# Two of three PSUM banks change owner, and the order of the attention steps is made anew

## What is computed

```python
q = rope((x @ Wq + bq).reshape(B, 512, 16, 16))       # 16 heads of 16
k = rope((x @ Wk + bk)[:, :, None, :])                # one key head for all
v = (x @ Wv + bv)[:, :, None, :]
att = softmax(where(causal, -inf, einsum('bthd,bThd->bhtT', q, k) / sqrt(16)))
x = x + ga * (einsum('bhtT,bThd->bthd', att, v).reshape(B, 512, 256) @ Wo + bo)
h = layernorm(x) * (1 + cb) + sb                      # and the router's logits of h
```

## Time and profile before

| | |
|---|---|
| median of 3 runs | 1330.33 us (1328.81 to 1330.93) |
| the profiled execution | 1328.92 us, of which 1327.0 us span |
| mean granted TensorE clock | 0.924 of full |
| attention, from the first transposes of the input to the last logits | 44.8 to 507.2 us |
| busy over the span | PE 84%, DVE 56%, ACT 43%, POOL 34% |

### The profile page before, as it was taken

The page is one execution under the profiler, slowest core; times in us unless marked ns, Lnnn a source line. Parts: engine busy times, 40 slices in busy tenths (PEclk is TensorE's granted clock), DMA queues, the critical chain, the costliest instruction groups (busy, mean ns, idle before and its releaser), DMA issues. The chain is left out here.

```text
span 1327.0 us, 19347 instructions
## 1 busy us (share of the span) xinstructions
PE 1121.3 (84%) x6462; PEld 593.2 (45%) x6462; DVE 744.3 (56%) x1538; ACT 566.0 (43%) x1025; POOL 457.4 (34%) x668
## 2 busy tenths in 40 slices
PE   6279999999999991598989638999999929999996
PEld 5134445554544430354545315666666613333332
DVE  3167778788787745223223237777777623464543
ACT  0227676676776661123223213333333204545543
POOL 0345446445454310478877523222223100000000
PEclk7669999999999995699999859999999969999997
DMA  4134134233252213266666430111110020012000
GB/s 169 30 58 77 26 70 93 46 75 85 39 90 58 43 50 105 72 128 155 130 151 132 75 99 1 37 37 37 37 41 17 21 91 1 8 56 64 0 32 32
DMA packets 73042, 85.26 MB, mean 64 GB/s; under 512 B 12520, under 2 KB 67560, under 8 KB 72688
## 3 DMA queue, kind: packets, MB, share of 16 engines
q1 hardware_dynamic: 60656, 67.23, 19.8%
q0 software_dynamic: 12288, 16.79, 7.7%
HBM read 45.54 MB, written 25.47 MB: 54 GB/s over the span
## 5 line engine op out<-in xcount | busy, mean ns | idle before, releaser
L655 DVE TENSOR_REDUCE nmax<-psum 128x1 f32<-128x512 f32 (+3 forms) x352 | 215.5, 636 | 51.9 <-PE psum L847 46.5
L759 ACT ACTIVATE pT<-psum 128x512 f32<-128x512 f32 x320 | 181.1, 596 | 66.7 <-PE psum L866 36.6
L845 PE MATMUL psum<-k6T,q6T 96*128 96x512 bf16 (+3 forms) x512 | 128.2, 310 | 14.3 <-DVE nmax L655 10.2
L863 PE MATMUL psum<-q6T,k6T 99*128 99x512 bf16 x320 | 119.4, 382 | 1.1 <-ACT pT L759 0.9
L1084 POOL DMA_INDIRECT residual<-expert_y,idx_e x64 | 101.2, 1581 | 37.6 <-DVE expert_y L1206 21.1
L2029 PE MATMUL psum<-c_state,c_w 128*128 128x512 f32 x192 | 102.5, 636 | 0.1
L847 PE MATMUL psum<-negs_bf,ident_bf 128*128 128x128 bf16 (+2 forms) x352 | 88.8, 252 | 0.0
L845 PEld LDWEIGHTS psum<-k6T,q6T 96*128 96x128 bf16 x512 | 45.7, 99 | 88.0 <-DVE nmax L655 55.5
L878 PE MATMUL psum<-pT,v 128*32 128x512 f32 x640 | 85.1, 604 | 0.0
L1487 DVE TENSOR_TENSOR l_scores<-psum,const_sb 128x512 f32<-128x512 f32 x128 | 79.1, 679 | 10.0 <-PE psum L1639 10.0
L1071 POOL DMA_INDIRECT expert_tokens<-router_input,idx_e x64 | 63.7, 995 | 54.3 <-POOLq L947 35.2
(11 more groups left out here) (234 smaller groups left out, 2259.1 us busy)
## 6 DMA issues: line engine op xcount, KB each, us to landing
q6T<-q_parts SPq DMA_DIRECT2D x96, 128.0 KB, 4.5
expert_w<-in_ew SPq DMA_DIRECT2D x16, 768.0 KB
x_in<-in_x SPq DMA_DIRECT2D x8, 512.0 KB, 4.0
residual<-x SPq DMA_DIRECT2D x32, 128.0 KB, 1.8
router_input<-h SPq DMA_DIRECT2D x32, 128.0 KB, 1.8
l_x<-residual SPq DMA_DIRECT2D x8, 512.0 KB, 4.2
x_dram<-l_x SPq DMA_DIRECT2D x32, 128.0 KB, 3.5
c_x<-x_dram SPq DMA_DIRECT2D x4, 1024.0 KB, 6.0
```

The lines of the kernel that those rows point to most:

```text
L655: dve.tensor_reduce(nmax[:, i, u * nh:(u + 1) * nh], ps_s[:, n % SR, 0:nh * (i + 1) * P].rearrange("p (h k) -> p h k", h=nh), AX_X, ALU.ma ...
L759: act.activation(pT[:, n % PR].rearrange("p h t -> p (h t)"), ps_t[:, n % TR, :], ACT.Exp, scale=HD ** -0.5).then_inc(probs, 1)
L845: pe.matmul(out[:, a, :], q6T[0:6 * HD, b % 2, u * nh + a, i * P:(i + 1) * P], k6T[0:6 * HD, b % 2, 0:w], start=a == 0, stop=False, skip_g ...
L863: last = pe.matmul(out, k6T[:, b % 2, j * P:(j + 1) * P], q6T[:, b % 2, hg * 4:hg * 4 + 4, i * P:(i + 1) * P], start=True, stop=j < i)
```

## The change

The numbers of banks become two for what ScalarE drains and one for what VectorE drains, and the whole table of positions is replaced. No instruction is added, removed or resized.

```diff
-    "Q": [-124, -99],
+    "Q": [-125, -80],
-    "kv": -94,
+    "kv": -104,
...
-    SR, TR, PR, XR, YR = 2, 2, 8, 1, 2
+    SR, TR, PR, XR, YR = 2, 2, 8, 2, 1
```

More of the change, by code:

```diff
@@ L160 @@
 PLACE = {
[L161 to L164, removed]
-    "kv": -94,
-    "Q": [-124, -99],
[L167 to L180, removed]
+    "ln": -211,
+    "st": -183,
+    "xn": -151,
+    "hT": [-142, -136],
+    "kv": -104,
+    "Q": [-125, -80],
+    "sp": [-115, -53],
+    "kT": -89,
+    "qd": [-92, -29],
+    "S": [[-41, -34, -12, -11], [-59, -51, -45, -27, -7, -5, 2, 3], [-62, -57, -50, -37, -28, -18, -17, 12, 18, 22, 25, 31, 33, 35, 38, 40], [-54, -39, -32, -22, 8, 16, 24, 28, 45, 48, 52, 55, 62, 63, 69, 72]],
+    "mT": [4, 15, 50, 80],
+    "ST": [[[20, 27, 29, 34]], [[36, 39, 43, 46], [51, 54, 57, 60]], [[64, 66, 70, 71], [75, 76, 78, 81], [88, 90, 94, 96]], [[98, 100, 103, 105], [111, 112, 116, 117], [123, 126, 132, 134], [137, 141, 143, 145]]],
+    "PV": [[42], [59, 67], [87, 92, 106], [122, 135, 150, 153]],
+    "oE": [53, 68, 110, 155],
+    "oT": [65, 73, 120, 162],
+    "oC": [93, 113, 128, 173],
+    "pr": [115, 127, 142, 185],
+    "h2": [133, 146, 177, 194],
+    "h2T": [166, 220, 237, 285],
+    "lg": 295,
 }
```

## The result

The changed kernel takes 1349.58 us (median of 4 runs, 1348.22 to 1349.95) against 1330.37 us of the kernel before (4 runs): a ratio of 1.0144, 95% interval 1.0127 to 1.0162. It is slower by 19.2 us. The profiled execution took 1348.22 us, its span is 1346.3 us (before: 1327.0).

The account below looks back on a forecast made before the run. TensorE was taken as the bound, its work unchanged, only pauses moving: group less old waits +8.2, kT +7.0, head +2.0, end -1.7, sum 15.5 on the profiled 1328.92; median 1345.8, stated as 1345, range 1333 to 1353.

Parts of the forecast that it names:

- The group behind the second Q: TensorE pauses after each second Q, behind the h2 pair held up by GpSimd: 3.16 us a sequence, 20.6 us in all.
- kT: Transposes of k wait for GpSimd's chain behind kv: 1.0 us late, seven times, +7.0 us.
- It adds nothing: Third tile's mT: its split becomes ready 1.4 us later, where PE also arrives 1.4 later, so no added cost.
- The old waits go: S waits for maxima in the old order, 1.77 us a sequence, 12.4 in seven, disappear; with the new group, +8.2.
- Head: Start of attention: q DMAs land at 86.1 and delay the second half's first S; +2.0 us, bounds 0 and 4.
- End: Last logits come 2.3 us earlier with two banks; PE work moved ahead costs about 0.6: -1.7 us, bounds 0 and -4.
- Rival 1: Behind the second Q, L689 beats L545, the group costs 1.63 us a sequence: about 1336.5 us; chance 0.16.
- Rival 2: Faster: pauses behind the second Q don't arise, group under 0.7 us a sequence, old waits gone: 1325 us; chance 0.09.
- Rival 3: Nothing measurable: group behind the second Q at 1.63 us and kT hidden: 1329.6 us; chance 0.06.
- Rival 4: Heavier: second half's q DMAs land after their first S, 1 to 2 us more per sequence: 1355 us; chance 0.09.
- The others fit too.: VectorE's single bank: besides Q before the next oT, the other fills are also drained before the next one.
- about nothing: Two banks for ScalarE's drains: PE hardly waits for that bank in the steady state, so little gain there.

Follow-up runs that it names:

- Experiment 1: Changed kernel with the last h2 at 191 instead of 194, its VectorE pair in front of the second Q's eviction: 1342.59 us, ratio 1.0067 to the kernel before.
- experiment 8: experiment 4 with mT of the last tile one ST later (81 instead of 80): 1329.55 us, ratio 0.9980 to the kernel before.
- Experiment 3: Changed kernel with kT alone four steps later (-89 to -85), mT where it was: 1350.63 us, ratio 1.0142 to the kernel before.
- experiment 6: Kernel before, old order, with the new banks (two for ScalarE's drains, one for VectorE's): 1361.24 us, ratio 1.0216 to the kernel before.
- experiment 5: Changed kernel's order with the old banks (one for ScalarE's drains, two for VectorE's): 1356.97 us, ratio 1.0192 to the kernel before.
- experiment 2: Changed kernel with kT (-89 to -85) and mT of the third tile (50 to 54) four steps later: 1342.29 us, ratio 1.0077 to the kernel before.
- experiment 9: experiment 8 with one S of the third tile (-50 to -48) behind a PV: 1327.00 us, ratio 0.9971 to the kernel before.
- experiment 4: Changed kernel with the edits of Experiment 1 and experiment 2 together: 1333.60 us, ratio 1.0004 to the kernel before.

## Why the prediction was right

The forecast was 1345 (1333 to 1353), measured are 1349.6: +19.2 us where 15 were forecast.

- **The group behind the second Q**, forecast 3.16 us a sequence, measured 2.59. The cause was read rightly: L686 to 0.29 behind L542, L689 lost to L545 by 0.04, all six times (ends at 5.08 and 6.63 behind the start of Q, forecast 5.03 and 6.57). Experiment 1 shows that the pair at this place is the cause. The third S started 7.29 behind the start of Q, where 7.30 was forecast; but TensorE wanted it only at 6.26 instead of 6.04, because the walk left out the small pauses in front of it, 0.1 at each of two PV among them. That is 0.23 of the 0.57 by which the group was too large. I gave 6 x 1.53 to L689, 9.2 us, and the cure brought 6 x 1.49; the two are near each other partly by luck, for the cure also took away the pair's own 0.95 us, and the rest, 1.63 by my walk, was 1.10. Where the walk had an S waiting 0.68, an ST waits 0.30 for L759. This wait and that of the mT come from elsewhere, since experiments 1 and 8 show them with an untroubled pair.
- **kT**, forecast 1.0 late, measured 1.29, seven times: 9.0 instead of 7.0. The period of 54.86 us lies in the forecast 54.5 to 55.
- **"It adds nothing" for mT of the third tile** was right for the changed kernel, where that mT shares kT's wait. Experiment 3 shows how little of it was slack: it takes the whole wait as soon as kT gives it up.
- **The old waits go**: they did, all 1.77. Both together, forecast +15.2 for seven sequences, measured 12.9 + 2.7 = +15.6. The smaller group and the larger kT nearly cancelled.
- **Head**, forecast +2.0, measured +2.0, and that is luck. The mechanism was half right: the first S of the second half does wait for q6T's DMA, 1.22 us, but the DMA lands by 84.7 instead of 86.1. The other part is a clock at 0.71 instead of 1.00 from 94 to 99 us, which the forecast didn't have. How long it lasts differs between executions: in experiment 1 the same instructions would have made the head's term +5.3.
- **End**: the tail behind the last PV is 2.1 shorter (forecast 2.3). The work moved ahead costs all of its 1.5 instead of 0.6: -0.6 instead of -1.7.
- **Behind attention** the forecast said nothing would change, and 2.4 us more arose (the next section but one). With it 2.0 + 15.6 - 0.6 + 2.4 = 19.4, where the spans differ by 19.3.

Rival 1, the pair that slips through, didn't occur. Rivals 2 and 3 needed a group under 0.7 us or a hidden kT, and neither came. Rival 4, late q DMAs in the steady state, has no row in the trace. Of the signs that the forecast named, the distance of the kT, the shorter tail, L689 long once in four and a wait for VectorE's bank before the second oT alone are there; of "three or four S" that L655 releases, the rows of the group show two. That the banks fit (*"The others fit too."*) held for the new order; experiment 6 shows the same bank count 2.55 us short in the old one. And that two banks for ScalarE give *"about nothing"* holds for the old order alone, in whose rows it was read: in the new one the second bank is worth 1.56 us a sequence (experiment 5).

## What to carry to other kernels

Read a change of an order by its neighbourhoods, not by its totals: here three numbers carry all of the 19 us, and each was to be seen in the rows of before (a VectorE pair directly behind a step that starts GpSimd work; a consumer 5.4 us of work behind a producer that needs 6.4). Put VectorE's work with two SBUF inputs where it waits for ScalarE anyway, ahead of GpSimd's long operations. And when a wait is taken away, look for what else hangs on the same late engine: the wait goes there whole unless that is moved too.

## What the runs showed of the hardware that I had not expected

**A clock that falls behind short waits.** In experiment 6 waits of 0.85 and 1.70 us some 6 us apart, with the clock at 1.00 through both, were followed in four sequences of six by a stretch at 0.50. The same waits at the same places left it at 1.00 in the two others. So the same 2.55 us of waiting cost a sequence between 2.7 and 6.0 us (55.29 and 58.52 less 52.57).

The head of the new order shows it again. In the changed kernel and the seven experiments with its order an S waits 1.95 us for L655, until 94.5 to 96.7 us. About the end of this wait the clock falls to 0.50 for 3.4 us in the changed kernel and experiments 2, 3, 8 and 9, for 13.7 us in experiments 1 and 4, and not at all in experiment 5. What decides between them isn't shown.

**The same code, a few microseconds apart.** From the last L787 to the end of the span all twelve kernels execute the same instructions, and the profiled executions took between 819.0 us (experiment 2) and 825.1 (experiment 8) for it; before 820.1, after 822.5. The windows view of that part, kernel before, changed kernel, experiments 2 and 8:

```profile
507.00:1327.00 820.00, 669.15 (x3570) 362.35 (x3570) 401.33 (x831) 269.47 (x448) 252.23 (x232) 0.92 0.25 62
```

```profile
524.00:1346.30 822.30, 671.44 (x3570) 362.55 (x3570) 401.19 (x831) 269.43 (x448) 251.92 (x232) 0.91 0.25 62
```

```profile
515.10:1333.70 818.60, 667.43 (x3570) 360.91 (x3570) 401.23 (x831) 269.27 (x448) 252.36 (x232) 0.92 0.25 62
```

```profile
505.70:1330.50 824.80, 673.94 (x3570) 364.51 (x3570) 401.48 (x831) 269.31 (x448) 251.40 (x232) 0.91 0.25 61
```

Counts are equal, VectorE, ScalarE and GpSimd are busy equally long to 1.0 us, and only TensorE's busy time moves, from 667.4 to 673.9. The records of the clock go with it, though not in every run: TensorE was at 0.50 for 137.5 us of this part in the kernel before, 143.3 in the changed one, 135.6 in experiment 2 and 149.3 in experiment 8. So the 2.4 us that the changed kernel loses there are within what executions of one code differ by. They are no effect of the change that could be shown, nor is it excluded: when the part starts was not varied by itself.
